# First sweep of a graph layer: two PSUM buffers for the support's product, and the first panel's degrees after fourteen tiles

## The chip, the cores and the metric

The kernel runs on one NeuronCore of a Trainium2 chip. The metric is the device time of one execution in microseconds (us). TensorE is called PE here, VectorE DVE, ScalarE ACT, GpSimd POOL, and SP is the engine whose queue issues nearly all DMAs.

## What is computed

Two graph-and-feed-forward layers on x (3327 rows of 256 fp32 numbers, padded to 26 tiles of 128) with a 3327 by 3327 matrix `adj`. The change lies in the first graph convolution:

```python
def _L0_gnn_ref(x, adj, W):
    A_hat = adj + jnp.eye(adj.shape[0], dtype=adj.dtype)
    d_inv_sqrt = jnp.sum(A_hat, axis=1) ** (-0.5)
    A_norm = d_inv_sqrt[:, None] * A_hat * d_inv_sqrt[None, :]
    support = x @ W.T
    out = A_norm @ support
    return jax.nn.relu(out)
...
x = x + _L0_gnn_ref(_layernorm(x, axis=-1), adj, L0_gnn_W)
```

After it come a routed feed-forward of 8 experts, a second graph convolution, and a feed-forward of 30 steps.

## The kernel before

`first_graph_block` reads the transposed matrix twice. The first sweep, which is where the change is, goes through 9 groups of rows q = 0 to 8 (eight panels of 3 tiles and a last one of 2); each panel has 13 chunks i = 0 to 12 of 384 KB, loaded into a ring `raw` of 11 slots by SP (L381, in `load`). SP issues load n when `free(n - 11)` says that the chunk which last used the slot has been read.

What each engine does in the first sweep, in the order written out in its program:

- DVE adds every chunk of a panel into a PSUM accumulator (`add_chunk`, L583 for a panel's first pair, L586 after that; even panels use `psT[:, 0:2]`, odd ones `acc[1]`). At chunk 4 of panel q it reads the degrees of panel q - 1 (`degrees`, L591 to L594), at chunk 7 it scales three tiles of support (`scale_s`, L600 and L604), and for chunks whose rows have been scaled it makes the low half of a split (`split_low`, L611).
- ACT copies a finished accumulator to `colsum` (`column_sum`, L459), makes the high halves (`split_high`, L473) and keeps a panel's partial product (`keep_part`, L468).
- PE turns the column sums into degrees (`degrees`, L908, and L911 where PE has added some chunks itself, L921), and multiplies split chunks by scaled support (`contract`, L931).
- POOL takes the power -0.5 of the degrees (`invert`, L842).

Beside this, during panels 0 and 1, the support is made, one tile t after another, by ACT and PE in turns. Step t of `support_steps` is: ACT normalises tile t (`normalise_x`, L441), copies the transposed tile t - 1 out of PSUM (`copy_xnT`, L448), and copies the product of tile t - 2 to `s_row` (`copy_support`, L452). PE transposes tile t (`turn_x`, L891), and multiplies tile t - 1 by the weights (`support`, L901). The transposes have two PSUM buffers (`psX`), the product has one (`psS`, in the bank of `psR`):

```python
                if t >= 1:
                    pe.wait_ge(sup_done, t)
                for k in range(KD):
                    last = pe.matmul(psS, xnT[:, t % 2, k, :], w[:, k, :], start=(k == 0), stop=(k == KD - 1))
```

so PE's product of tile t waits until ACT has copied that of tile t - 1. Steps 0 to 17 belong to panel 0, steps 18 to 27 to panel 1's chunks 0 to 9. ACT takes panel 0's `column_sum` at chunk 1 of panel 1 (behind step 18), PE its `degrees` at chunk 2 (behind step 19, which multiplies tile 18). Contraction of panel 1 begins at its chunk 11, on PE behind a wait for all 26 tiles of support, and on ACT (L473) behind the last copy of support.

Of the kernel before, what the change touches and what calls it, by code (L numbers as in the profile page):

```python
# [25 lines left out]
ACT = mybir.ActivationFunctionType  # L26
# [7 lines left out]
D = 256  # L34
KD = D // P
# [8 lines left out]
PT = 3  # L44
# [5 lines left out]
CHUNKS = NT // CT  # L50
# [129 lines left out]
def first_graph_block(nc, g, x_in, w0, adjt, adjl, s_row, route):  # L180


    with ExitStack() as ctx:
# [14 lines left out]
        w = sb("g0_w", [P, KD, D])  # L198
        xn = sb("g0_xn", [P, 2, D])
        xnT = sb("g0_xnT", [P, 2, KD, P])  # L200
# [38 lines left out]
        psT = ps("g0_psT", [P, PT, 512])  # L239
        psR = ps("g0_psR", [P, 512])  # L240
# [1 line left out]
        deg_acc = [psT[:, 0:CT, :], acc[1]]  # L242
        psD = psT[:, PT - 1, 0:NT]
        psX = [acc[0][:, b, 0:D].rearrange("p (k n) -> p k n", k=KD) for b in range(2)]
        psS = psR[:, 0:D]
        psP = psR[:, 0:PANEL]

        filled, placed = sem("filled"), sem("placed")
# [5 lines left out]
        xn_done, xtr_done, xnT_done, xmm_done, sup_done = (sem(n) for n in ("xn", "xtr", "xnT", "xmm", "sup"))  # L254
        dve_added, pe_added = sem("dve_added"), sem("pe_added")
        colsum_done, deg_mm, deg_added, deg_done = sem("colsum"), sem("deg_mm"), sem("deg_added"), sem("deg")
# [12 lines left out]
        def tiles_of(q):  # L269
            return list(range(q * PT, min(q * PT + PT, NT)))  # L270
# [30 lines left out]

        def support_steps(q, i):
            if q == 0:
                return [i] if i < 8 else [2 * i - 8, 2 * i - 7]
            return [18 + i] if q == 1 and i < 10 else []


        def part_of(q):
# [12 lines left out]
        def item(q, i):  # L321
            return q * CHUNKS + i
# [40 lines left out]
        def early_before(q, i):  # L363
            return before1(q) + sum(len(early(q, a)) for a in range(i))
# [71 lines left out]
        def _(act):  # L436
# [12 lines left out]

            def copy_support(t):  # L450
                act.wait_ge(xmm_done, t + 1)
                act.activation(s_row[:, t, :], psS, ACT.Copy).then_inc(sup_done, 1)  # L452

            def column_sum(q):
                v = width(q)
# [51 lines left out]
            for q in range(GROUPS):  # L507
                for i in range(CHUNKS):
                    n = item(q, i)
                    if i == 1 and q >= 1:  # L510
                        column_sum(q - 1)
                    if i == 2 and q >= 2:
                        keep_part(q - 1)
                    if early(q, i):
                        act.wait_ge(loaded[n % RING], n // RING * 16 + 16)
                    for a, j in enumerate(early(q, i)):
                        split_high(early_before(q, i) + a, n, j % CT, width(q))
                    for t in support_steps(q, i):
                        if t < NT:
                            normalise_x(t)  # L520
                        if 1 <= t <= NT:
                            copy_xnT(t - 1)
                        if t >= 2:
                            copy_support(t - 2)
# [360 lines left out]
        def _(pe):  # L885
# [8 lines left out]
            def support(t):  # L894
                if t == 0:
                    pe.wait_ge(w_loaded, 16)
                pe.wait_ge(xnT_done, t + 1)
                if t >= 1:
                    pe.wait_ge(sup_done, t)
                for k in range(KD):  # L900
                    last = pe.matmul(psS, xnT[:, t % 2, k, :], w[:, k, :], start=(k == 0), stop=(k == KD - 1))  # L901
                last.then_inc(xmm_done, 1)

            def degrees(q):
                pe.wait_ge(colsum_done, q + 1)
                for i, t in enumerate(tiles_of(q)):
                    for a in range(CT):
                        last = pe.matmul(psD[:, t:t + 1], colsum[:, a, i * P:(i + 1) * P], g.ones[:, 0:1], start=(a == 0),  # L908
                                         stop=(a == CT - 1 and not PE_SUMS[q]))
                    if PE_SUMS[q]:  # L910
                        last = pe.matmul(psD[:, t:t + 1], rowsum[0:1, i * P:(i + 1) * P], g.ones[0:1, 0:1], start=False,  # L911
                                         stop=True)
                last.then_inc(deg_mm, 1)
# [61 lines left out]

            for q in range(GROUPS):
                for i in range(CHUNKS):
                    if i == 2 and q >= 1:
                        degrees(q - 1)
                    if i in pe_places(q):  # L980
                        add_chunk(q, i)
                    for a, j in enumerate(early(q, i)):
                        if j == 0 and q >= 2:
                            pe.wait_ge(part_done, q - 1)
                        if j == 0 and q == 1:
                            pe.wait_ge(sup_done, NT)
                        if j % PT == 0:
                            pe.wait_ge(sl_done, j // PT + 1)
                        contract(early_before(q, i) + a, acc[0], j, width(q), j == 0, j == q * PT - 1)
                    for t in support_steps(q, i):  # L990
                        if t < NT:
                            turn_x(t)
                        if 1 <= t <= NT:
                            support(t - 1)
            for m in range(END):
                if m == 1:
                    degrees(GROUPS - 1)
                if m < TURNS:
                    k, j = PLACE[m], row_tile(m)
# [1194 lines left out]
```

## Time and profile before

| | us |
|---|---|
| median of 3 runs | 1946.84 (1945.93 to 1947.46) |
| the profiled execution, its own time | 1950.9 |
| its span | 1949.1 |
| busy in the span: PE, DVE, ACT, POOL | 1807.9, 1616.5, 1331.3, 959.1 |
| issued loads of `raw` in panels (384 KB), number and median time to landing | 168, 4.8 |

The profile gives for each engine its busy time, and a trace of every instruction with what ended the idle time before it. The first sweep of the first graph layer fills roughly the first 218 us of the span. A matrix product that the program issues once stands as two matmuls in the trace (fp32), so the two products of one tile are four L901 rows. "Granted clock" is the share of full speed that PE's clock was let run at.

### The profile page before, as it was taken

How to read it: one execution, taken by the hardware profiler on the slowest of the kernel's cores; microseconds unless marked ns; L12 is line 12 of the kernel's file. 1: busy time of each engine (PE TensorE's matmuls, PEld its weight loads, DVE VectorE, ACT ScalarE, POOL GpSimd, SP SyncE). 2: the span in 40 equal slices, each digit the busy share in tenths (PEclk: the TensorE clock that was granted, in tenths of full speed). 3: DMA queues.
4: the chain of work that ended last, by engine and by line, in shares of the span. 5: the costliest groups of instructions: out<-in, count | busy, mean ns of one | idle time of the engine just before them, and what ended most of it. 6: DMA issues, size and time to landing. Idle time of an engine off the chain costs nothing. (4 is left out here: it accounts for less than half of the span.)

```text
span 1949.1 us, 41788 instructions
## 1 busy us (share of the span) xinstructions
PE 1807.9 (93%) x12680; PEld 1702.0 (87%) x12680; DVE 1616.5 (83%) x4226; ACT 1331.3 (68%) x2651; POOL 959.1 (49%) x1703
## 2 busy tenths in 40 slices
PE   6799999829999999858999979999999999999997
PEld 4689999829999999857888869999999999999997
DVE  5689878739999999738656559999999999999996
ACT  4434555416666666543555459999999999999995
POOL 2000134535555555530101027777777777777774
PEclk8889999959999999979999999999999999999999
DMA  8676778237887887543556400000000000000002
GB/s 310 207 250 201 218 200 179 96 136 215 233 234 232 236 237 228 133 170 104 193 173 203 143 17 2 2 2 2 2 1 2 2 2 2 2 2 2 2 2 71
DMA packets 97235, 226.26 MB, mean 116 GB/s; under 512 B 20897, under 2 KB 51363, under 8 KB 88620
## 3 DMA queue, kind: packets, MB, share of 16 engines
q1 hardware_dynamic: 82476, 206.33, 33.8%
q0 software_dynamic: 14592, 17.91, 4.7%
q8 instruction: 80, 1.31, 0.3%
q14 instruction: 87, 0.71, 0.1%
HBM read 204.43 MB, written 19.75 MB: 115 GB/s over the span
## 5 line engine op out<-in xcount | busy, mean ns | idle before, releaser
L2028 PE MATMUL ffn_psH<-ffn_w2h,ffn_vTh 128*128 128x256 f32 x1320 | 393.0, 298 | 1.5 <-DVE ffn_u L2084 1.5
L2028 PE MATMUL ffn_psH<-ffn_w2h,ffn_vTl 128*128 128x256 f32 x1320 | 374.3, 284 | 0.0
L2028 PE MATMUL ffn_psH<-ffn_w2l,ffn_vTh 128*128 128x256 f32 x1320 | 373.9, 283 | 0.0
L2117 POOL TENSOR_SCALAR ffn_vn<-ffn_vn,ffn_rstd,ffn_shift 128x256 f32<-128x256 f32 x540 | 300.0, 560 | 21.1 <-issue 1.2
L2072 DVE BATCH_NORM_STATS2 ffn_stats<-ffn_vn 128x6 f32<-128x256 f32 x780 | 284.5, 406 | 25.0 <-ACT ffn_vn L2054 23.9
L2084 DVE SCALAR_TENSOR_TENSOR ffn_u<-ffn_th,ffn_psH 128x512 f32<-128x512 f32 x390 | 263.5, 676 | 7.4 <-ACT ffn_th L2051 7.4
L2028 PEld LDWEIGHTS ffn_psH<-ffn_w2h,ffn_vTh 128*128 128x128 f32 x1320 | 253.0, 192 | 2.5 <-DVE ffn_u L2084 1.7
L2028 PEld LDWEIGHTS ffn_psH<-ffn_w2l,ffn_vTh 128*128 128x128 f32 x1320 | 253.2, 192 | 0.8
L2028 PEld LDWEIGHTS ffn_psH<-ffn_w2h,ffn_vTl 128*128 128x128 f32 x1320 | 252.5, 191 | 0.0
L2054 ACT ACTIVATE ffn_vn<-ffn_u 128x512 f32<-128x512 f32 x390 | 248.7, 638 | 0.8 <-DVE ffn_u L2084 0.8
L2051 ACT ACTIVATE ffn_th<-ffn_psH 128x512 f32<-128x512 f32 x390 | 232.6, 596 | 1.7 <-PE ffn_psH L1991 1.7
L2077 DVE TENSOR_TENSOR ffn_vTl<-ffn_psT,ffn_vTh 128x512 fp32r<-128x512 f32 x330 | 222.1, 673 | 3.6 <-ACT ffn_vTh L2045 3.6
L2009 PE MATMUL ffn_psT<-ident,ffn_vn 128*128 128x128 f32 x1560 | 214.7, 275 | 10.0 <-POOL ffn_vn L2117 9.8
L2045 ACT ACTIVATE ffn_vTh<-ffn_psT 128x512 fp32r<-128x512 f32 x330 | 195.9, 594 | 27.1 <-PE ffn_psH L2028 17.2
L2009 PEld LDWEIGHTS ffn_psT<-ident,ffn_vn 128*128 128x128 f32 x1560 | 175.0, 141 | 27.4 <-POOL ffn_vn L2117 23.1
L1738 ACT ACTIVATE moe_hr<-moe_psH,moe_b 128x256 f32<-128x256 f32 x264 | 110.8, 471 | 126.0 <-PE moe_psH L1846 117.0
L2123 POOL TENSOR_TENSOR ffn_rstd<-ffn_veps,mhalf 128x4 f32<-128x4 f32 x195 | 196.4, 1007 | 0.1
L931 PE MATMUL g_acc<-g_hi,g_sh 128*128 128x384 f32 (+1 forms) x468 | 162.6, 347 | 12.0 <-DVE g_lo L611 6.8
L473 ACT ACTIVATE g_hi<-g_raw 128x384 fp32r<-128x384 f32 (+1 forms) x234 | 111.6, 508 | 88.7 <-PE g_acc L931 71.5
L1364 DVE TENSOR_TENSOR g_lo<-g_raw,g_hi 128x512 fp32r<-128x512 f32 (+1 forms) x182 | 114.3, 649 | 67.2 <-ACT g_hi L1307 66.8
L1307 ACT ACTIVATE g_hi<-g_raw 128x512 fp32r<-128x512 f32 (+1 forms) x182 | 105.2, 597 | 91.1 <-PE g_acc L1492 90.1
L2060 ACT ACTIVATE ffn_vn<-ffn_vn,ffn_shift,ffn_rstd 128x256 f32<-128x256 f32 x240 | 144.4, 602 | 26.7 <-POOL ffn_shift L2127 24.5
(240 smaller groups left out, 5021.6 us busy)
## 6 DMA issues: line engine op xcount, KB each, us to landing
g_raw<-in_adjt SPq DMA_DIRECT2D x168, 384.0 KB, 4.8
g_raw<-in_wide SPq DMA_DIRECT2D x78, 512.0 KB, 3.7
moe_w1raw<-in_wall SPq DMA_DIRECT2D x33, 1024.0 KB, 5.2
moe_w2raw<-in_wall SPq DMA_DIRECT2D x33, 1024.0 KB, 5.9
moe_b<-in_eb SPq DMA_DIRECT2D x33, 128.0 KB, 4.5
g_raw<-in_adjl SPq DMA_DIRECT2D x14, 256.0 KB, 2.8
g_raw<-in_narrow SPq DMA_DIRECT2D x13, 256.0 KB, 2.6
xn_rows<-rt_hn SPq DMA_DIRECT2D x8, 384.0 KB, 4.2
```

Source lines behind the costliest of these rows:

```text
L931: last = pe.matmul(to[:, d, 0:v], s[:, j, fs], a[:, b, 0:v], start=(first and r == 0), stop=(last_one and r == 2))
L2009: last = pe.transpose(psT[w % R][:, q * KD + k, :], vn[:, gr * Q + q, k * P:(k + 1) * P], g.ident[:])
L2028: last = pe.matmul(psH[w % R][:, q * D:(q + 1) * D], a[:, w % R, q * KD + k, :], b[:, k, :], start=(k == 0 and j == 0), stop=(k == KD - 1 ...
L2045: act.activation(to[:, m % R], psT[m % R][:], ACT.Copy).then_inc(copied, 1)
L2051: act.activation(th[:, a], psH[a][:], ACT.Tanh).then_inc(th_done, 1)
L2054: act.activation(vn[:, tiles(m - SILU)].rearrange("p q d -> p (q d)"), u[:, (m - SILU) % R], ACT.Silu).then_inc(v_done, 1)
L2060: act.activation(vn[:, t, :], vn[:, t, :], ACT.Identity, scale=rstd[:, s:s + 1], bias=shift[:, s:s + 1]).then_inc(vn2_done, 1)
L2072: last = dve.bn_stats(stats[:, t, :], vn[:, t, :])
L2077: dve.tensor_tensor(vTl[:, w % R], psT[w % R][:], vTh[:, w % R].bitcast(F32), ALU.subtract).then_inc(lo_done, 1)
L2084: dve.scalar_tensor_tensor(out=u[:, a], in0=th[:, a], scalar=0.01, in1=psH[a][:], op0=ALU.mult, op1=ALU.add).then_inc(u_done, 1)
L2117: last = pool.tensor_scalar(vn[:, t, :], vn[:, t, :], rstd[:, s:s + 1], shift[:, s:s + 1], ALU.mult, ALU.add)
L2123: pool.tensor_tensor(rstd[:, q], veps[:, q], g.mhalf[:, 0:2 * Q], ALU.pow).then_inc(rstd_done, 1)
```

## The change

The product of the support gets a second PSUM buffer, `psS = (psR[:, 0:D], psT[:, PT - 1, D:2 * D])`; even tiles use the first, odd tiles the second, and PE's product of tile t waits for ACT's copy of tile t - 2 in place of t - 1. The second buffer lies in the bank in which `psD`, the degrees, lies. For that, PE takes the degrees of panel 0 only when 14 tiles (0 to 13) have been copied, and the product of an odd tile from 15 on waits until DVE has read those degrees. Step 13 and 14 now come at chunk 0 of panel 1, two steps a chunk go on to chunk 3, and one a chunk to chunk 10. ACT takes panel 0's `column_sum` at chunk 0 of panel 1, ahead of step 13, and PE takes its degrees at chunk 1, behind step 14. In the new file the lines of the support and of what follows stand 6 to 10 lines further down.

```diff
--- before.py
+++ after.py
@@ -242,7 +242,8 @@
         deg_acc = [psT[:, 0:CT, :], acc[1]]
         psD = psT[:, PT - 1, 0:NT]
         psX = [acc[0][:, b, 0:D].rearrange("p (k n) -> p k n", k=KD) for b in range(2)]
-        psS = psR[:, 0:D]
+
+        psS = (psR[:, 0:D], psT[:, PT - 1, D:2 * D])
         psP = psR[:, 0:PANEL]
 
         filled, placed = sem("filled"), sem("placed")
@@ -301,8 +302,13 @@
 
         def support_steps(q, i):
             if q == 0:
-                return [i] if i < 8 else [2 * i - 8, 2 * i - 7]
-            return [18 + i] if q == 1 and i < 10 else []
+                return [i]
+            if q == 1 and i < 11:
+                return [CHUNKS + 2 * i, CHUNKS + 2 * i + 1] if i < 4 else [CHUNKS + 4 + i]
+            return []
+
+
+        AHEAD_OF_DEGREES = CHUNKS + 1
 
 
         def part_of(q):
@@ -449,7 +455,7 @@
 
             def copy_support(t):
                 act.wait_ge(xmm_done, t + 1)
-                act.activation(s_row[:, t, :], psS, ACT.Copy).then_inc(sup_done, 1)
+                act.activation(s_row[:, t, :], psS[t % 2], ACT.Copy).then_inc(sup_done, 1)
 
             def column_sum(q):
                 v = width(q)
@@ -507,7 +513,7 @@
             for q in range(GROUPS):
                 for i in range(CHUNKS):
                     n = item(q, i)
-                    if i == 1 and q >= 1:
+                    if i == (0 if q == 1 else 1) and q >= 1:
                         column_sum(q - 1)
                     if i == 2 and q >= 2:
                         keep_part(q - 1)
@@ -895,14 +901,18 @@
                 if t == 0:
                     pe.wait_ge(w_loaded, 16)
                 pe.wait_ge(xnT_done, t + 1)
-                if t >= 1:
-                    pe.wait_ge(sup_done, t)
+                if t >= 2:
+                    pe.wait_ge(sup_done, t - 1)
+                if t % 2 and t >= AHEAD_OF_DEGREES:
+                    pe.wait_ge(deg_added, 1)
                 for k in range(KD):
-                    last = pe.matmul(psS, xnT[:, t % 2, k, :], w[:, k, :], start=(k == 0), stop=(k == KD - 1))
+                    last = pe.matmul(psS[t % 2], xnT[:, t % 2, k, :], w[:, k, :], start=(k == 0), stop=(k == KD - 1))
                 last.then_inc(xmm_done, 1)
 
             def degrees(q):
                 pe.wait_ge(colsum_done, q + 1)
+                if q == 0:
+                    pe.wait_ge(sup_done, AHEAD_OF_DEGREES)
                 for i, t in enumerate(tiles_of(q)):
                     for a in range(CT):
                         last = pe.matmul(psD[:, t:t + 1], colsum[:, a, i * P:(i + 1) * P], g.ones[:, 0:1], start=(a == 0),
@@ -975,7 +985,7 @@
 
             for q in range(GROUPS):
                 for i in range(CHUNKS):
-                    if i == 2 and q >= 1:
+                    if i == (1 if q == 1 else 2) and q >= 1:
                         degrees(q - 1)
                     if i in pe_places(q):
                         add_chunk(q, i)
```

PE's order before, around the degrees of panel 0 (L891 the transposes, L901 the product, L908 the degrees; each row with "x5" or without is so many instructions, and `g_psR` is the PSUM tile of the product):

```order
L901 MATMUL g_psR<-g_w,g_xnT 128x256 [waits g0_sup,g0_xnT]
L901 MATMUL g_psR<-g_w,g_xnT 128x256
L908 MATMUL g_psT<-ones,g_colsum 128x1 [waits g0_colsum]
L908 MATMUL g_psT<-ones,g_colsum 128x1 x5
L891 MATMUL g_acc<-ident,g_xn 128x128 [waits g0_xnT,g0_xn]
L891 MATMUL g_acc<-ident,g_xn 128x128
L901 MATMUL g_psR<-g_w,g_xnT 128x256 [waits g0_sup,g0_xnT]
L901 MATMUL g_psR<-g_w,g_xnT 128x256
```

The same place in the changed kernel (L897 the transposes, L909 the product, L918 the degrees):

```order
L909 MATMUL g_psT<-g_w,g_xnT 128x256 [waits g0_sup,g0_xnT]
L909 MATMUL g_psT<-g_w,g_xnT 128x256
L918 MATMUL g_psT<-ones,g_colsum 128x1 [waits g0_sup,g0_colsum]
L918 MATMUL g_psT<-ones,g_colsum 128x1 x5
L897 MATMUL g_acc<-ident,g_xn 128x128 [waits g0_xnT,g0_xn]
L897 MATMUL g_acc<-ident,g_xn 128x128
L909 MATMUL g_psR<-g_w,g_xnT 128x256 [waits g0_sup,g0_xnT]
L909 MATMUL g_psR<-g_w,g_xnT 128x256
L897 MATMUL g_acc<-ident,g_xn 128x128 [waits g0_xnT,g0_xn]
L897 MATMUL g_acc<-ident,g_xn 128x128
L909 MATMUL g_psT<-g_w,g_xnT 128x256 [waits g0_deg_added,g0_sup,g0_xnT]
L909 MATMUL g_psT<-g_w,g_xnT 128x256
```

The degrees stood behind the products of 19 tiles and now stand behind those of 14, with a wait for their copies; the products alternate between two tiles of PSUM, and that of tile 15 has a further wait for DVE's reading of the degrees.

ACT's order in the changed kernel, at the boundary from panel 0 to panel 1 (L447 normalises, L454 copies the transposes, L458 the product, L465 the column sums):

```order
L447 ACTIVATE g_xn<-x,g_negshift,g_rstd 128x256 [waits g0_xtr,g0_norm0]
L454 ACTIVATE g_xnT<-g_acc 128x256 [waits g0_xmm,g0_xtr]
L458 ACTIVATE l_s<-g_psR 128x256 [waits g0_xmm]
L465 ACTIVATE g_colsum<-g_psT 128x768 [waits g0_dve_added]
L447 ACTIVATE g_xn<-x,g_negshift,g_rstd 128x256 [waits g0_xtr,g0_norm0]
L454 ACTIVATE g_xnT<-g_acc 128x256 [waits g0_xmm,g0_xtr]
L458 ACTIVATE l_s<-g_psT 128x256 [waits g0_xmm]
```

Before, the copy of the column sums stood behind 19 normalised tiles (0 to 18); now it stands behind 13 (0 to 12), and still waits for DVE's last addition of panel 0. The orders of DVE, POOL and SP are the same in both kernels.

## Rows read from the trace of the kernel before

**Rows 1.** Windows: length, busy PE, PEld, DVE, ACT, POOL; granted clock, DMA share, GB/s

```profile
19.80:29.80 10.00, 9.08 (x23) 6.06 (x24) 7.62 (x31) 5.19 (x14) 0.85 (x1) 0.50 1.03 406
29.80:49.00 19.20, 15.37 (x71) 11.07 (x69) 10.54 (x11) 12.78 (x34) 4.18 (x11) 1.00 0.80 278
49.00:66.00 17.00, 12.71 (x62) 9.31 (x62) 9.63 (x18) 10.97 (x29) 0.85 (x1) 1.00 0.45 139
74.50:77.60 3.10, 3.10 (x11) 3.10 (x10) 3.06 (x8) 0.56 (x2) 0.00 (x0) 0.50 0.49 138
88.00:101.50 13.50, 12.49 (x39) 11.18 (x40) 9.14 (x19) 4.27 (x9) 0.85 (x1) 0.50 0.88 309
```

**Rows 2.** Waits from 28 to 66: us in total, times, longest

```profile
PE g_psR L901 <- ACT l_s L452: 6.6, 19, 0.6
```

**Rows 3.** Timeline of DVE: start, us, work, count, [idle before and its releaser]

```profile
28.77 8.46 DVE L586 TENSOR_TENSOR g_psT<-g_psT,g_raw 128x768 f32<-128x768 f32 x8
...
53.43 0.16 DVE L591 TENSOR_SCALAR g_deg<-g_psT 128x3 f32<-128x3 f32 x1 [12.12 <-PE g_psT L908]
...
58.88 4.17 DVE L586 TENSOR_TENSOR g_acc<-g_acc,g_raw 128x768 f32<-128x768 f32 x4
65.40 1.03 DVE L611 TENSOR_TENSOR g_lo<-g_raw,g_hi 128x384 fp32r<-128x384 f32 x2 [2.35 <-ACT g_hi L473]
...
90.05 0.97 DVE L583 TENSOR_TENSOR g_acc<-g_raw 128x768 f32<-128x768 f32 x1 [7.07 <-issue]
```

**Rows 4.** Timeline of ACT

```profile
30.46 0.38 ACT L452 ACTIVATE l_s<-g_psR 128x256 f32<-128x256 f32 x1 [1.08 <-PE g_psR L901]
30.74 0.59 ACT L441 ACTIVATE g_xn<-x,g_negshift,g_rstd 128x256 f32<-128x256 f32 x1
31.24 0.37 ACT L448 ACTIVATE g_xnT<-g_acc 128x256 f32<-128x256 f32 x1
...
49.08 0.81 ACT L459 ACTIVATE g_colsum<-g_psT 128x768 f32<-128x768 f32 x1
49.77 0.60 ACT L441 ACTIVATE g_xn<-x,g_negshift,g_rstd 128x256 f32<-128x256 f32 x1
...
64.57 0.38 ACT L452 ACTIVATE l_s<-g_psR 128x256 f32<-128x256 f32 x1 [1.28 <-PE g_psR L901]
64.85 1.34 ACT L473 ACTIVATE g_hi<-g_raw 128x384 fp32r<-128x384 f32 x3
```

**Rows 5.** Timeline of PE

```profile
20.31 0.69 PE L891 MATMUL g_acc<-ident,g_xn 128*128 128x128 f32 x2 [3.94 <-ACT g_xn L441]
...
23.55 2.04 PE L901 MATMUL g_psR<-g_w,g_xnT 128*128 128x256 f32 x4
25.39 0.63 PE L891 MATMUL g_acc<-ident,g_xn 128*128 128x128 f32 x2
...
30.99 1.10 PE L901 MATMUL g_psR<-g_w,g_xnT 128*128 128x256 f32 x4 [0.35 <-ACT l_s L452]
31.93 0.38 PE L891 MATMUL g_acc<-ident,g_xn 128*128 128x128 f32 x2
...
52.00 1.40 PE L908 MATMUL g_psT<-ones,g_colsum 128*128 128x1 f32 x12
53.25 0.42 PE L891 MATMUL g_acc<-ident,g_xn 128*128 128x128 f32 x2
53.50 1.03 PE L901 MATMUL g_psR<-g_w,g_xnT 128*128 128x256 f32 x4
54.37 0.38 PE L891 MATMUL g_acc<-ident,g_xn 128*128 128x128 f32 x2
...
63.43 1.10 PE L901 MATMUL g_psR<-g_w,g_xnT 128*128 128x256 f32 x4 [0.56 <-ACT l_s L452]
...
73.95 0.41 PE L931 MATMUL g_acc<-g_hi,g_sh 128*128 128x384 f32 x1 [1.94 <-DVE g_lo L611]
```

**Rows 6.** Loads of L381 that were issued from 0 to 90

```profile
DMA to landing us min/median/max: 3.1/8.1/13.9
```

## The prediction

> **What bounds the kernel now.** I read the timelines of DVE, ACT and PE over the first 90 us first, since the change touches only panels 0 and 1 of the first sweep, then the windows for the clock and the transfers, and last the loads. The question is which chain ends last before the first contraction on PE, because from there on all engines wait for one another.
>
> It is the chain of the support. DVE is through with panel 0 at 28.77 + 8.46 = 37.23, adds four more times, and then stands idle for 12.12 us, until 53.43, for the degrees, which PE makes behind the products of 19 tiles [rows 3, 5]. It is still not the one that is late: from 53.43 it has 9.6 us of work (to 58.88 + 4.17 = 63.05), and then waits another 2.35 us for ACT's high halves [rows 3], which ACT begins behind its last copy of support, at 64.57 [rows 4]. So the two waits are 14.5 us of idle DVE, but the chain of the support decides the moment 65.40 at which the work of panel 1 goes on.
>
> That chain runs in turns. PE waits 19 times, 6.6 us in all, for ACT's copy of the product [rows 2]. One turn: the copy starts at 30.46 and takes 0.38, the product starts 0.15 later at 30.99 and takes 1.10 [rows 4, 5], and the next copy starts 0.04 after it (63.43 + 1.10 = 64.53, copy at 64.57). Sum 0.38 + 0.15 + 1.10 + 0.04 = 1.67 us a tile. The transfers do not bind here: the queues fall from 278 to 139 GB/s in the second half of this stretch, as DVE frees no slot while it waits [rows 1].
>
> **The change, part by part.**
>
> *Two buffers.* The product of a tile no longer waits for the copy just before. Three bounds are left. PE alone: transposes at 53.25, product at 53.50, next transposes at 54.37, 1.12 us a tile [rows 5] (the other product rows give 31.93 - 30.99 = 0.94 in place of 0.87, so up to 1.19). ACT alone: 0.28 from copy to normalising, 0.50 from there to the copy of the transposes [rows 4], and some 0.28 for that one, 1.06. The loop through both over two tiles: 0.28 + 0.50 + 0.37 + 0.15 + 1.10 + 0.04 = 2.44, that is 1.22 us a tile. It is the longest of the three, so I take 1.22; 1.12 stays as the lower end, 1.67 (nothing gained) as the upper. At the low clock, where a product with its gap takes 25.39 - 23.55 = 1.84 and the transposes some 0.5 (twice 0.25), a tile takes 2.34.
>
> *Before the hand-over this is worth nothing on the path.* ACT now copies the column sums ahead of step 13, and that copy waits for DVE, whose end at 37.23 nothing moves. With 1.22 us a tile, ACT and PE have done steps 0 to 12 by about 37.2 (PE's transposes of tile 7 about 29.6, five more steps bring 35.9, the product behind them ends about 37.3); so the support arrives there as DVE ends. ACT waits some 1 us and PE some 1.3 us for it. This is a new wait, and behind it on ACT stand step 13 and all later ones: it is what the 5 tiles gained so far are spent on.
>
> *From the hand-over on.* Column sums 37.25, normalising 0.69 later at 37.94 (49.77 - 49.08 [rows 4]), copy of tile 12's transposes at 38.44, end 38.81, product of tile 12 at 38.96; product of tile 13 after 0.94 and 0.25 at 40.15, end 41.25, its copy 41.29 to 41.67; degrees on PE at 41.82. They hold PE for 53.25 - 52.00 = 1.25 us, and DVE reads them 1.43 us after their start (53.43 - 52.00), so at 43.25, **10.2 us earlier** than before. DVE is ready then (it has waited since 41.3), so the new wait of tile 15's product on DVE's reading, done at 43.4, is over before PE is there (tile 14's product starts at 43.32 and takes longer). I cost it at nothing; the cover is tile 14's product, and if it were gone the price would be some 0.2 us, once.
>
> *The rest of the support.* Product of tile 14 at 43.32, eleven more at 1.22 put that of tile 25 at 56.7, end 57.8, its copy 57.9 to 58.2, where it was 64.57 to 64.95. **The chain ends 6.7 us earlier.** With 1.12 a tile it would be 7.8, with 1.35 5.3.
>
> *DVE.* Degrees at 43.25 plus 9.6 us gives 52.9; it then waits about 5.9 us for ACT's high halves in place of 2.35. So 10.2 us come on DVE, 3.5 of them are given back in this wait, and 6.7 stay. Its additions need chunks that landed before 46, and slots freed earlier let SP issue its next loads 10 us earlier, in a stretch where the queues have room [rows 1]; the next slot that SP needs is then one that only the contraction frees. SP and POOL have the same order as before; POOL's powers have tens of us of slack.
>
> *After that* every engine stands where it stood at 65.40, 6.7 us earlier, with the same loads in the ring; what follows is the same sequence. Sum: -6.7 us. The profiled execution took 1950.9 us (span 1949.1), which would make 1944.2; it lay 4.1 us above the median of the runs, so against the median of 1946.84 the forecast is **1940.1 us**. A measurement of this kernel can tell about 0.2% from no change, 3.9 us.
>
> **A rule that speaks against it.** The rows say that PE waits for the copies, 0.35 us a tile [rows 5], at full clock. The Trainium skill (TensorE: Matmul & The Clock Gate, section HAM oscillation — how this bites in real kernels) reports of a matmul kernel, once its loop order was mended, that double-buffering PSUM gave no further gain. By that the sum would be 0 and the time 1946.8; this trace, with 6.6 us of such waits, disagrees, and the case that no gain comes is rival E.
>
> **The rivals.**
>
> *A. The clock halves at the new hand-over.* After 3.94 us of idle PE ran at 0.50 (its level of 1.2 GHz) for 10 us, after 1.94 us for 3.1 us, and once for 13.5 us [rows 1, 5]. The new gaps are 1.3 us and 0.6 us: against. Price: in a low stretch a tile takes 2.34 in place of 1.22, so 48% of it is lost: 1.5 us for 3.1, 4.8 for 10, 6.5 for 13.5. Time 1941.6 to 1946.6, at its middle 1945.
>
> *B. It ends slower.* The mechanism is the same, but kept up: PE's short gaps between products keep its clock at 1.2 GHz to the end of the support. From tile 12's product at 38.96, thirteen more tiles at 2.34 (30.4), 2.5 for the degrees, about 0.5 for their wait and 2.5 from the last product's start to its copy's end bring 74.9, 9.9 us later than 64.95: 1957. It decides from a low stretch of 6.7 / 0.48 = 14 us on. Against: from 29.8 to 66 the clock was 1.00 with larger gaps than the change leaves [rows 1]. The Trainium skill (TensorE: Matmul & The Clock Gate, section A second HAM failure mode: psum-queue depth-cycling) tells of a kernel whose cycling through PSUM banks made the clock swing between its levels in just this way; no row here shows it.
>
> *C. The transfers take it back.* At 83 to 90 DVE waits 7.07 us [rows 3] for chunks that took up to 13.9 us to land [rows 6]. If they came at the same moment as before, all 6.7 us would go into a longer wait: 1946.8. Against: SP issues them as slots come free, and that moves too.
>
> *D. More than the sum.* The low stretch from 88 to 101.5, in which PE is busy for 12.49 of 13.50 us [rows 1], falls otherwise or is shorter; at full clock up to half of that busy time goes, of which DVE would see perhaps 4 us: 1936.
>
> *E. It doesn't do what it says:* another wait keeps a tile at 1.67; only the degrees move, DVE waits for ACT instead, 1946.8.
>
> **How the numbers follow.** Forecast 0.65 (its own range 1938.5 to 1942, from 1.12 and 1.35 us a tile and the scatter of the runs), A 0.12, B 0.04, C 0.07, D 0.08, E 0.04. Faster by over 0.2% (below 1942.9): forecast, D and a quarter of A, 0.76. Same: most of A, C and E, 0.20. Slower: B, 0.04. The range leaves out B, most of C and E, and the ends of A and D: 1936 to 1945.
>
> **What would show it.** In the changed profile: products of the support 1.2 us apart with no wait for the copy two before; DVE's degrees at about 43; the last copy of support at about 58; DVE's first low half near 58.8 after a wait of about 6 us; and PE's clock at 1.00 from 30 to 59. Every later landmark, the wait for chunks at 83 to 90 first, should stand 6 to 7 us earlier. The forecast is wrong if tiles stay above 1.4 us apart, if the clock falls at 38 to 45, or if the wait for chunks grows by what was gained.

## The result, and the profile after

| | before | changed |
|---|---|---|
| median, us (lowest to highest) | 1947.03 (1943.36 to 1949.59, 20 runs) | 1942.66 (1939.01 to 1948.35, 20 runs) |
| ratio | | 0.9981, 95% interval 0.9974 to 0.9989 |
| profiled execution, its span, us | 1950.9, 1949.1 | 1943.88, 1942.1 |

The change gains 4.4 us by the medians (2.1 to 5.1 by the interval). It is faster beyond doubt, but at 0.19% it sits right at the bound of what one measurement tells. The forecast was a gain of 6.7 us and 1940.1 us. One thing is odd at once: the changed kernel scatters over 9.3 us, and the kernel before over 6.2.

Lines of the changed kernel stand 6 to 10 further down than in the rows of before: product L909, PE's transposes L897, degrees L918, ACT's copy of the support L458, high halves L479, DVE's low halves L617. The timeline of PE (start, us, work, [idle before and its releaser]), from the first tiles to the end of the support, answers to [rows 5]:

```profile
20.47 0.69 PE L897 MATMUL g_acc<-ident,g_xn 128*128 128x128 f32 x2 [4.70 <-ACT g_xn L447]
...
33.60 0.38 PE L897 MATMUL g_acc<-ident,g_xn 128*128 128x128 f32 x2
33.81 1.03 PE L909 MATMUL g_psT<-g_w,g_xnT 128*128 128x256 f32 x4
38.78 0.44 PE L897 MATMUL g_acc<-ident,g_xn 128*128 128x128 f32 x2 [3.93 <-ACT g_xn L447]
39.05 1.46 PE L909 MATMUL g_psR<-g_w,g_xnT 128*128 128x256 f32 x4
40.30 0.64 PE L897 MATMUL g_acc<-ident,g_xn 128*128 128x128 f32 x2
40.73 1.91 PE L909 MATMUL g_psT<-g_w,g_xnT 128*128 128x256 f32 x4
43.21 1.47 PE L918 MATMUL g_psT<-ones,g_colsum 128*128 128x1 f32 x12 [0.56 <-ACT l_s L458]
...
45.88 1.03 PE L909 MATMUL g_psT<-g_w,g_xnT 128*128 128x256 f32 x4
46.78 0.44 PE L897 MATMUL g_acc<-ident,g_xn 128*128 128x128 f32 x2
47.06 1.13 PE L909 MATMUL g_psR<-g_w,g_xnT 128*128 128x256 f32 x4
48.02 0.38 PE L897 MATMUL g_acc<-ident,g_xn 128*128 128x128 f32 x2
48.24 1.03 PE L909 MATMUL g_psT<-g_w,g_xnT 128*128 128x256 f32 x4
...
57.48 1.03 PE L909 MATMUL g_psT<-g_w,g_xnT 128*128 128x256 f32 x4
```

Two tiles take 48.24 - 45.88 = 2.36 us, 1.18 each, and no product waits for a copy any more. But at the hand-over PE stands idle for 3.93 us, and the two products behind that take 1.46 and 1.91 us and not 1.03 to 1.13. From 44.50 to 57.50 PE is busy for all of the 13.00 us: now PE itself sets the 1.18 us a tile. In the first stretch tile 7 is turned at 27.62, 2.0 us earlier than I forecast. The windows (busy PE, PEld, DVE, ACT, POOL; then granted clock, DMA share, GB/s) show why:

```profile
34.00:39.30 5.30, 1.37 (x7) 0.84 (x7) 4.88 (x6) 2.05 (x6) 0.31 (x1) 1.00 0.97 319
39.30:42.60 3.30, 3.30 (x10) 2.11 (x9) 1.96 (x3) 1.87 (x5) 0.00 (x0) 0.56 0.96 352
44.50:57.50 13.00, 13.00 (x69) 10.12 (x69) 9.04 (x16) 11.07 (x30) 0.85 (x1) 1.00 0.72 238
88.00:101.50 13.50, 13.50 (x56) 12.42 (x56) 12.18 (x24) 4.35 (x9) 0.85 (x1) 0.77 0.71 242
```

Behind the idle time the clock is granted at 0.56, which is nearly all at the lower level of 1.2 GHz, and then it is back. ACT's timeline has the other side of the same wait, for DVE's sums of panel 0, and the end of the support, [rows 4]:

```profile
33.80 0.38 ACT L458 ACTIVATE l_s<-g_psR 128x256 f32<-128x256 f32 x1
37.43 0.81 ACT L465 ACTIVATE g_colsum<-g_psT 128x768 f32<-128x768 f32 x1 [3.25 <-DVE g_psT L592]
...
58.54 0.38 ACT L458 ACTIVATE l_s<-g_psT 128x256 f32<-128x256 f32 x1 [0.48 <-PE g_psT L909]
58.82 1.34 ACT L479 ACTIVATE g_hi<-g_raw 128x384 fp32r<-128x384 f32 x3
```

And DVE's timeline, [rows 3]:

```profile
28.93 8.46 DVE L592 TENSOR_TENSOR g_psT<-g_psT,g_raw 128x768 f32<-128x768 f32 x8
...
44.71 0.16 DVE L597 TENSOR_SCALAR g_deg<-g_psT 128x3 f32<-128x3 f32 x1 [3.25 <-PE g_psT L918]
...
50.17 4.17 DVE L592 TENSOR_TENSOR g_acc<-g_acc,g_raw 128x768 f32<-128x768 f32 x4
59.37 1.03 DVE L617 TENSOR_TENSOR g_lo<-g_raw,g_hi 128x384 fp32r<-128x384 f32 x2 [5.03 <-ACT g_hi L479]
...
83.80 0.97 DVE L589 TENSOR_TENSOR g_acc<-g_raw 128x768 f32<-128x768 f32 x1 [6.87 <-issue]
```

The degrees come 8.7 us earlier than in [rows 3], the first low half 6.0 (65.40 to 59.37), and the wait for chunks in panel 3 has moved along by 6.2 and is as long as it was.

### The profile page after: what moved, and what is told of

Its sections match the earlier page's. It is cut to its first block and busy times, and to the rows that moved or that the text cites. A ratio compares the mean times of both kernels' runs of the same rounds, so it can differ in the third digit from the quotient of the medians.

```text
span 1942.1 us, 41788 instructions
## 1 busy us (share of the span) xinstructions
PE 1801.2 (93%) x12680; PEld 1698.4 (87%) x12680; DVE 1616.5 (83%) x4226; ACT 1330.7 (69%) x2651; POOL 961.5 (50%) x1703
## 5 line engine op out<-in xcount | busy, mean ns | idle before, releaser
L479 ACT ACTIVATE g_hi<-g_raw 128x384 fp32r<-128x384 f32 (+1 forms) x234 | 111.6, 508 | 88.1 <-PE g_acc L941 70.8
```

## The experiments

Three questions: which half of the change (two buffers, or the earlier hand-over, where ACT takes panel 0's column sums and PE its degrees) brings the gain; whether the idle time at the hand-over costs, by the clock or by the wait itself; and why the gain is smaller than the 6.0 us by which the landmark (DVE's first low half) moved. Each edit is shown against the changed kernel, with what it leaves alone marked by `...`.

**The order alone** (one buffer, the early hand-over):

```
-        psS = (psR[:, 0:D], psT[:, PT - 1, D:2 * D])
+        psS = (psR[:, 0:D], psR[:, 0:D])
...
-                if t >= 2:
-                    pe.wait_ge(sup_done, t - 1)
-                if t % 2 and t >= AHEAD_OF_DEGREES:
-                    pe.wait_ge(deg_added, 1)
+                if t >= 1:
+                    pe.wait_ge(sup_done, t)
...
-                if q == 0:
-                    pe.wait_ge(sup_done, AHEAD_OF_DEGREES)
```

> The change with one PSUM buffer for the product: column sums ahead of step 13 on ACT, degrees behind 14 tiles, but PE waits for the copy just before, 1.67 us a tile. Theory (the two buffers bring the whole gain, the order none): degrees read by DVE near 45.5, but last copy of support at 64.9 and first low half at 65.4 as before, and a median within 1.5 us of the kernel before. Rival (the order brings part of the gain, as DVE's additions and SP's loads come 8 us sooner): median 2 us or more below before.

Measured: 1945.78 us against 1945.38 before, ratio 1.0003 (0.9994 to 1.0011): no gain. DVE has its degrees at 42.78, 2.7 us earlier than expected, and hands all of it back in the wait for ACT. (Its first low half is at 63.08 and not at the expected 65.4; that is a matter of where this execution began the support, see the table below.)

```profile
42.78 0.16 DVE L597 TENSOR_SCALAR g_deg<-g_psT 128x3 f32<-128x3 f32 x1 [2.93 <-PE g_psT L914]
...
63.08 1.03 DVE L617 TENSOR_TENSOR g_lo<-g_raw,g_hi 128x384 fp32r<-128x384 f32 x2 [10.68 <-ACT g_hi L479]
```

**The buffers alone** (the old steps, column sums and degrees at their old places), twice:

```
-                return [i]
-            if q == 1 and i < 11:
-                return [CHUNKS + 2 * i, CHUNKS + 2 * i + 1] if i < 4 else [CHUNKS + 4 + i]
-            return []
+                return [i] if i < 8 else [2 * i - 8, 2 * i - 7]
+            return [18 + i] if q == 1 and i < 10 else []
-        AHEAD_OF_DEGREES = CHUNKS + 1
+        AHEAD_OF_DEGREES = 19
...
-                    if i == (0 if q == 1 else 1) and q >= 1:
+                    if i == 1 and q >= 1:
...
-                    if i == (1 if q == 1 else 2) and q >= 1:
+                    if i == 2 and q >= 1:
```

> Two buffers, hand-over where it stood before (column sums behind step 18 on ACT, degrees behind step 19 on PE). Theory (the support now reaches the new hand-over 3.3 us before DVE, so ACT and PE stand idle there, 3.25 and 3.93 us, and the clock falls after it): with no such idle time the tiles run through at 1.17 us, degrees read by DVE near 46, last copy of support near 55, first low half near 55.6 (59.4 in the changed kernel), no low clock between 30 and 55, and a median near 1938, 4 us below the changed kernel. Rival (the early hand-over is what brings the gain, as in the prediction): DVE gets its degrees later than 50, and the median is 1943 or more.

Measured: 1937.56 us, ratio 0.996 (0.9947 to 0.9974), that is 8.5 us below before and more than the whole change brings. PE has no idle time of 3 to 4 us: the largest in this stretch are 0.38 before tile 19's turn and 0.57 before the degrees, and the first low half starts at 55.97. One thing expected did not hold: the clock fell all the same, at 45.5, for 3.4 us.

```profile
42.04 0.44 PE L895 MATMUL g_acc<-ident,g_xn 128*128 128x128 f32 x2 [0.38 <-ACT g_xn L445]
```

```profile
45.52 0.16 DVE L595 TENSOR_SCALAR g_deg<-g_psT 128x3 f32<-128x3 f32 x1 [3.94 <-PE g_psT L916]
...
55.97 1.03 DVE L615 TENSOR_TENSOR g_lo<-g_raw,g_hi 128x384 fp32r<-128x384 f32 x2 [0.83 <-ACT g_hi L477]
```

So the two buffers carry the gain, and the earlier hand-over costs a part of it.

**The hand-over three steps later** (behind step 15 rather than step 12; the rest as changed):

```
-                return [i]
+                return [i] if i < 10 else [2 * i - 10, 2 * i - 9]
             if q == 1 and i < 11:
-                return [CHUNKS + 2 * i, CHUNKS + 2 * i + 1] if i < 4 else [CHUNKS + 4 + i]
+                return [16, 17] if i == 0 else [17 + i]
...
-        AHEAD_OF_DEGREES = CHUNKS + 1
+        AHEAD_OF_DEGREES = 17
```

> Hand-over three tiles later than in the change (column sums ahead of step 16 on ACT, degrees behind 17 tiles and step 17). Theory: ACT and PE wait less than 0.7 us at the hand-over, degrees read by DVE near 43.6, last copy of support near 55, first low half near 55.5, median near 1938, equal to the kernel with buffers alone. Rival (the place of the hand-over is indifferent): as the changed kernel, 1942 to 1943.

Measured: 1938.3 us, ratio 0.9959 (0.9945 to 0.9973). The idle time of 3.93 us has become 0.39, the first low half is at 55.14, and the clock stays at 1.00:

```profile
39.26 0.44 PE L897 MATMUL g_acc<-ident,g_xn 128*128 128x128 f32 x2 [0.39 <-ACT g_xn L447]
```

```profile
38.00:43.00 5.00, 4.05 (x23) 2.94 (x22) 3.46 (x4) 4.47 (x12) 0.00 (x0) 1.00 0.94 349
43.00:57.00 14.00, 12.36 (x67) 9.78 (x67) 10.88 (x20) 9.73 (x26) 0.85 (x1) 1.00 0.78 266
```

**The idle time filled** (the changed order; PE repeats its two transposes of tile 12 fourteen times in place of standing idle, so the wait for DVE is still there, but PE is busy in it; the helper `transposes` takes the tile, the number of times and whether to signal, and its definition is left out here):

```
+                        if t == CHUNKS - 1:
+                            transposes(t, 14, True)
```

> The changed kernel with 13 more transposes of tile 12 on PE, in the time in which PE waits for the hand-over (about 3.1 us of work in 3.9 us of idle time), the same values written again. Theory (the clock falls after the idle time and this costs about 1.5 us in the profiled run, more in the third of the executions that lie near 1947): clock 1.00 from 38 to 43, first low half near 58 in place of 59.4, median near 1939.5, and the executions near 1947 become rare. Rival (the slow third comes from elsewhere): the median falls by 1.5 us or less and the spread stays at 9 us.

Measured: 1939.1 us, ratio 0.9965 (0.9952 to 0.9979). PE is busy for 3.22 us of the wait, 0.64 remains, and the clock does not fall:

```profile
34.68 3.22 PE L900 MATMUL g_acc<-ident,g_xn 128*128 128x128 f32 x28
38.54 0.44 PE L900 MATMUL g_acc<-ident,g_xn 128*128 128x128 f32 x2 [0.64 <-ACT g_xn L447]
38.82 1.13 PE L913 MATMUL g_psR<-g_w,g_xnT 128*128 128x256 f32 x4
```

```profile
38.00:58.00 20.00, 17.79 (x94) 13.80 (x94) 12.19 (x21) 16.29 (x45) 0.86 (x1) 1.00 0.74 269
```

**The changed kernel and the one before, again.** One profile each is not enough in a stretch where the clock swings, so both were profiled again.

> The changed kernel once more, for its spread and a second profile. Theory: two groups of executions, near 1940 and near 1947; if this profile lies in the upper one, the low clock behind the hand-over or later in the first sweep lasts longer than the 3.3 us of the first profile. Rival: one group around 1942.7, the two groups were chance.

Measured: 1942.99 us, ratio 0.9989 (0.9978 to 0.9999). Four of 11 executions lie from 1945.33 up; the profiled one, 1942.99, shows a fall of 3.4 us behind 4.29 us of idle time.

> The kernel before once more, for a second profile of it. Theory (the execution profiled first lay high by chance, and part of its excess over the median lies in the stretch to 237 us, in the clock behind the wait for chunks): first low half again at 65.4, PE's first transposes of the result (g_out_t) at 233 to 235 in place of 237.0, time within 1 us of the median of the other runs. Rival: 237 again, the difference between the gain of the profiles (7.0) and of the medians (4.4) comes from behind the first graph layer.

Measured: 1946.6 us, ratio 1.0003 (0.9994 to 1.0012), as it must be. Its profile took 1944.75 us, 6.1 less than the one on which the prediction was built, and the difference lies in the stage that the change touches:

```profile
49.62 0.16 DVE L591 TENSOR_SCALAR g_deg<-g_psT 128x3 f32<-128x3 f32 x1 [10.08 <-PE g_psT L908]
61.60 1.03 DVE L611 TENSOR_TENSOR g_lo<-g_raw,g_hi 128x384 fp32r<-128x384 f32 x2 [2.35 <-ACT g_hi L473]
```

```profile
19.00:23.00 4.00, 3.68 (x10) 2.67 (x11) 2.71 (x7) 1.94 (x6) 0.00 (x0) 0.57 1.04 417
23.00:61.00 38.00, 30.38 (x144) 21.96 (x142) 24.46 (x52) 24.87 (x65) 5.88 (x12) 1.00 0.75 268
```

The first low half is at 61.60, not at 65.40. PE began tile 3 at 18.54 in place of 20.31, and the clock was low for 3.4 us in place of 10 [rows 1]. My expectation of 65.4 for it was wrong.

> The changed kernel a third time, beside the kernel before and the order alone on the same chip. Theory (scatter of the clock behind the hand-over and in the first sweep): first low half between 59.3 and 59.8 whenever the low stretch there is 3.3 us, later by 0.5 us for each us that it is longer; median 3 to 5 us below before. Rival: first low half the same to 0.2 us in all profiles, so that the scatter of 9 us comes wholly from later stages.

Measured: 1940.65 us, ratio 0.9975 (0.9963 to 0.9987). Its profiled execution took 1946.08 us and shows what the others don't: the clock stays low for 13.5 us behind the idle time, to the middle of the second panel's support.

```profile
37.09 0.69 PE L897 MATMUL g_acc<-ident,g_xn 128*128 128x128 f32 x2 [4.39 <-ACT g_xn L447]
37.57 1.91 PE L909 MATMUL g_psR<-g_w,g_xnT 128*128 128x256 f32 x4
...
39.70 1.91 PE L909 MATMUL g_psT<-g_w,g_xnT 128*128 128x256 f32 x4
42.18 2.69 PE L918 MATMUL g_psT<-ones,g_colsum 128*128 128x1 f32 x12 [0.56 <-ACT l_s L458]
```

```profile
36.00:49.50 13.50, 11.85 (x39) 9.58 (x40) 7.78 (x14) 6.11 (x16) 0.86 (x1) 0.51 0.75 271
```

```profile
61.96 1.03 DVE L617 TENSOR_TENSOR g_lo<-g_raw,g_hi 128x384 fp32r<-128x384 f32 x2 [7.43 <-ACT g_hi L479]
```

By now 43 executions of the changed kernel lay in two bands, up to about 1942 and from 1943 on, with five of them close about that bound (1942.76 to 1943.10). The last measurement put it beside its two counterparts on one chip.

> The changed kernel once more, beside the two that follow on the same chip. Its 43 executions so far lie in two bands, about 1937 to 1942 and 1943 to 1948. My theory: the upper band is executions whose clock stays at its lower level for long after the new idle time at the hand-over (36 to 50 us in the one profile that took 1946.1), so both bands should show again, with a median of 1940 to 1943. A rival: the bands are the scatter that every kernel has; then the next two kernels should scatter as widely, over 8 us or more.

Measured: 1941.19 us, ratio 0.998 (0.9968 to 0.9992). Nine of 12 lie between 1938.13 and 1942.88, three between 1947.58 and 1948.48.

> Two buffers with the old order of the hand-over, once more. My theory: it has no idle time of 3 to 4 us on PE at 37, so no execution lies in the upper band: median 1937 to 1939, all below 1942. If the early hand-over costs nothing and the difference seen before was chance, its median stands within 2 us of the changed kernel's.

Measured: 1939.65 us (1937.32 to 1941.67), ratio 0.9963 (0.995 to 0.9976). None in the upper band; the median is 0.7 above what I expected, and in this measurement only 1.5 below the changed kernel's, which by my own bound of 2 us would leave the rival standing. In the first pair of measurements the distance was 5.4 us, and over all executions (below) it is 3.0.

> The changed order with PE's idle time at the hand-over filled by repeated transposes of tile 12 (the same values, written again). My theory, the clock: no upper band, median 1938 to 1940.5, granted clock 1.00 from 30 to 58. The rival, that the wait itself costs (ACT and PE stand for DVE) and not the clock: it should look as the changed kernel does, upper band included, since the wait for DVE is still there.

Measured: 1941.36 us (1937.89 to 1943.12, 8 runs), ratio 0.9968 (0.9958 to 0.9979): the median is 0.9 above the expected span, and no lower than that of the changed kernel in the same measurement, 1941.19. The earlier pair had 1939.1 against 1942.99. So the medians leave the price of the fall at anything from nothing to 3.9 us. The granted clock reads 1.00 throughout this stretch, as expected, and even in the one before it:

```profile
19.00:36.00 17.00, 15.32 (x78) 12.28 (x79) 13.77 (x38) 11.25 (x30) 5.54 (x14) 1.00 0.98 363
36.00:58.00 22.00, 19.12 (x107) 14.91 (x105) 14.10 (x23) 16.95 (x45) 0.85 (x1) 1.00 0.79 273
```

For the earlier stretch the instructions contradict that column. Two products there take as long as they do at the lower level in the other profiles:

```profile
20.84 1.91 PE L913 MATMUL g_psR<-g_w,g_xnT 128*128 128x256 f32 x4
...
22.97 1.41 PE L913 MATMUL g_psT<-g_w,g_xnT 128*128 128x256 f32 x4
```

From 24.43 on every product takes 1.03 to 1.13, so behind the hand-over the clock was up by both signs.

All executions together, from every measurement:

| | executions | median, us | above 1943 | from 1945 up |
|---|---|---|---|---|
| before | 95 | 1946.3 | 89 | 68 |
| order alone | 11 | 1945.8 | 11 | 6 |
| changed | 55 | 1941.9 | 22 | 17 |
| idle time filled | 13 | 1940.1 | 1 (1943.12) | 0 |
| two buffers alone | 10 | 1938.9 | 0 | 0 |
| hand-over behind step 15 | 5 | 1938.3 | 0 | 0 |

The gap in the changed kernel's executions lies between 1943.88 and 1945.33, and the first profiled execution, 1943.88, shows the short fall, so the last column is the better count: 38 executions below it with a median of 1940.7, 17 above with 1947.55. Were the bands the same for all, none of these 17 would fall among the 28 of the last three kernels about three times in 10,000. Within the two measurements that had both, the counts are 4 of 11 against 0 of 15 and 3 of 12 against 0 of 13, which chance alone would bring about twice in 1,000 (all worked out from the counts). So the upper band belongs to the idle time at the hand-over.

The granted clock of whole executions points the same way: it is 0.962 to 0.965 in the 17 (mean 0.9631) and 0.965 to 0.971 in the 38 (mean 0.9667). By an estimate, a difference of 0.0036 over 1945 us is some 14 us more at half the clock. It doesn't say where in the execution they lie, and a mean of 0.964 alone does not put an execution into the upper band: one of each of the other three kernels has it, at 1941.57 to 1942.95.

Where each profiled execution stood, in us (the turn of g_out_t is PE's first transposes of the layer's result; DVE's idle time before the landmark in brackets; the last column is the span less the column before it):

| | execution | PE's turn of tile 3 | degrees read | first low half | first turn of g_out_t | rest |
|---|---|---|---|---|---|---|
| before | 1950.9 | 20.31 | 53.43 [12.12] | 65.40 [2.35] | 237.0 | 1712.1 |
| before again | 1944.75 | 18.54 | 49.62 [10.08] | 61.60 [2.35] | 232.2 | 1710.8 |
| order alone | 1946.05 | 18.83 | 42.78 [2.93] | 63.08 [10.68] | 233.2 | 1711.1 |
| changed | 1943.88 | 20.47 | 44.71 [3.25] | 59.37 [5.03] | 229.8 | 1712.3 |
| again | 1942.99 | 20.59 | 45.05 [3.49] | 59.71 [5.04] | 229.9 | 1711.3 |
| third | 1946.08 | 18.79 | 44.91 [5.13] | 61.96 [7.43] | 233.3 | 1711.0 |
| fourth | 1941.95 | 20.10 | 44.47 [3.39] | 59.13 [5.03] | 228.6 | 1711.6 |
| filled | 1940.07 | 20.24 | 43.10 [1.87] | 57.76 [5.04] | 226.6 | 1711.7 |
| filled again | 1943.12 | 20.36 | 43.24 [1.87] | 57.90 [5.03] | 228.1 | 1713.3 |
| buffers alone | 1937.21 | 20.58 | 45.52 [3.94] | 55.97 [0.83] | 225.4 | 1710.1 |
| and again | 1941.67 | 20.12 | 45.28 [4.18] | 56.82 [1.92] | 227.9 | 1712.0 |
| hand-over 16 | 1941.57 | 20.78 | 43.82 [2.05] | 55.14 [1.71] | 226.8 | 1713.0 |

From the first low half to the turn of g_out_t it is 168.8 to 171.7 us everywhere, and the rest is 1710.1 to 1713.3: what the change gains or loses is settled by the first low half, and some 3 us of scatter in either stretch come on top, whatever the kernel. (So the hand-over behind step 15 has the earliest landmark, 55.14, and an execution of 1941.57.)

The column of tile 3's turn matters too. Three of these executions began it at 18.5 to 18.8, the others at 20.1 to 20.8, and DVE's sums of panel 0 moved with it (they end at 35.5 and 35.7 in the second profile of before and the third of the changed kernel, at 37.2 and 37.4 in the first ones). So landmarks are compared from tile 3's turn. From there the first low half comes 45.1 and 43.1 us later in the kernel before, 44.3 in the order alone, 38.9 to 39.1 in the changed kernel's three short cases, 43.2 in its long one, 37.5 with the idle time filled, 35.4 and 36.7 with the buffers alone, and 34.4 with the hand-over behind step 15.

**The constants.** In every kernel above DVE stands idle for some 7 us in panel 3. Behind it are four small transfers (zeros, the slot table, two router tensors) that SP issues between the loads of panels 2 and 3. One edit, on top of the two buffers alone, moves them a panel ahead, between the loads of panels 1 and 2:

```
-                if q == 2:
+                if q == 1:
                     constants()
```

> Two buffers with the hand-over where it stood before (as the kernel e1), and SP issues the four small transfers of constants behind panel 1's loads in place of panel 2's, near 39 to 43 us, where DVE waits for its degrees. Theory (DVE's wait of 7 us for chunks in panel 3 comes from these transfers, which stand ahead of panel 3's first loads): the wait of 6.99 us at 80.5 falls under 2 us, and the median lies 4 to 6 us below e1, near 1933. Rival (the wait comes from the ring, whose slots come free late in panel 2): it stays at 5 us or more and the median within 1.5 us of e1.

Measured: 1929.9 us, ratio 0.9918 (0.9905 to 0.9931), 7.7 below the same kernel without the edit (6.9, when each is taken against the kernel before of its own measurement), and 3 us lower than I expected. The wait of 7 us is gone; one of 1.77 us at 57.85 is new. DVE's timeline, first of the kernel with the buffers alone, then of this one:

```profile
80.54 0.97 DVE L587 TENSOR_TENSOR g_acc<-g_raw 128x768 f32<-128x768 f32 x1 [6.99 <-issue]
```

```profile
57.85 0.97 DVE L587 TENSOR_TENSOR g_psT<-g_raw 128x768 f32<-128x768 f32 x1 [1.77 <-issue]
...
72.02 0.96 DVE L587 TENSOR_TENSOR g_acc<-g_raw 128x768 f32<-128x768 f32 x1
```

Of the 8.5 us between the two starts 2.1 are the earlier turn of tile 3 in this execution (18.45 for 20.58), so the edit is worth some 6.4 there. The two summaries of the transfers from 60 to 80 us, the same two kernels in the same order, say what filled the time:

```profile
DMA packets 2260, 4.69 MB, mean 235 GB/s; under 512 B 594, under 2 KB 850, under 8 KB 2259
```

```profile
DMA packets 2304, 6.32 MB, mean 316 GB/s; under 512 B 252, under 2 KB 252, under 8 KB 2303
```

As many packets, but a third more bytes: with the constants in this stretch many of the packets are small. Which of the four transfers it is, and whether their packets or their issue on SP (3.4 us from 61.76 to 65.18) cost more, I did not try apart.

**The best of both** (hand-over behind step 15, constants early):

> The hand-over behind step 15 (e3_handover_16) and the four small transfers of constants a panel earlier (e8_constants_early). If the two gains stand beside each other: 1938.3 less the 7.7 us between e8 and e1, about 1930.6, no wait of 7 us at 80. If the constants only helped with the old order of the hand-over: about 1938.

Measured: 1931.01 us, ratio 0.9917 (0.9904 to 0.993), 7.3 below the hand-over behind step 15 without the edit (8.2, each against its own before), as expected, and the wait of 7 us is gone here too. It does no better than the buffers alone with constants early: that one is 15.5 us and this one 16.0 us below the kernel before the change, each in its own measurement.

## Why the prediction was right, and where it was off

**Two buffers make a tile take 1.22 us and not 1.67: right.** Measured 1.18. But the bound was misnamed: PE is busy for 13.00 of 13.00 us there, so it is PE alone (1.12 to 1.19 in my own working) and not the loop through ACT (1.22). What the Trainium skill reports of its kernel (TensorE: Matmul & The Clock Gate, section HAM oscillation — how this bites in real kernels), that double-buffering PSUM gave no further gain, does not carry over to this one: alone it brings 0.996 and 0.9963, the largest effect of the change. Rival E is out.

**The support's chain decides, not the degrees: right, and shown.** With the order alone the degrees come 6.8 us earlier than in the profile of before that began tile 3 at nearly the same time (42.78 for 49.62), and nothing is gained.

**"Before the hand-over this is worth nothing on the path": right, with a price that I missed.** The step that failed is the one behind it: the support "arrives there as DVE ends", so that ACT waits some 1 us and PE 1.3. It arrived 3.3 us early. I had taken over the low clock up to 29.8 from the one profile; in the changed kernel the clock was up at 26, which brought tile 7's turn 2.0 us forward, and 1.18 us a tile did the rest. ACT waited 3.25 to 3.95 us, and PE 3.93, 4.29, 4.39 and 4.30 in the four profiles. This opened rival A, which I had priced well (a gain cut to 1941.6 to 1946.6) and given only 0.12 on the ground of gaps that were three times too small. The clock fell in all four profiles: for 3.4 us in three, for some 13.5 in the third.

**What the fall costs.** From tile 3's turn to the first low half, the short case takes 38.9 to 39.1 us and the filled kernel 37.5: 1.4 to 1.6 us. The long case takes 43.2, which is 5.6 more than the filled kernel. Rival A had 1.5 for 3.1 us of low clock and 6.5 for 13.5, so its prices were near. The long case stands 4.1 to 4.3 us behind the short one; the bands are 6.8 apart. That the upper band of executions is this long case rests on one profile of it, on this size, which covers the greater part of the distance, and on the granted clocks above; the rest of the distance has no source on record. That the band is absent without the idle time rests on 28 executions. The filled kernel still waits for DVE's sums, and its first low half comes 0.9 to 2.8 us behind those of the kernels that hand over later: the wait itself costs too, and no less than a short fall.

**The sum of 6.7 us: mis-sized by where it was measured from.** The landmark came out near what I had (58.8 forecast; 59.1 to 59.7 in three profiles), and the profiled execution of the changed kernel took 1943.88 us where the sum made 1944.2. But I carried the sum over to the medians as if the 4.1 us by which that profile of before lay above its median would be in the changed kernel too. Part of them lay inside this very stage: 10 us of low clock against 3.4 in the second profile, and a tile 3 that began 1.8 us later. The two are not alike. The later start is one that either kernel feels, since DVE's sums move with it. The longer low clock, some 2.0 us of the landmark (45.1 less 43.1), is one that the changed kernel does not feel: it lies ahead of the hand-over, where ACT and PE have 3 to 4 us to spare. So, from tile 3's turn, the change gains 6.0 to 6.2 us in the short case against the profile on which the prediction was built, 3.9 to 4.2 against the second one, and against that one nothing in the long case (43.2 for 43.1). The gain of the medians, 4.4, is a mixture of these. That the landmark came out so near its 58.8 is in part luck: without the fall it stands at 57.8 and 57.9 (filled kernel), 0.9 to 1.0 earlier than I had, and the fall that I had not counted put it back by some 1.5.

**DVE's new wait of 5.9 us for the high halves:** 5.03, and 7.43 in the long case. **The degrees at 43.25:** 44.5 to 45.1, late by the low clock; 43.10 and 43.24 in the filled kernel, where it stayed up, so the turn-by-turn sum was right.

**Rival C** (the loads take it back) is out: the wait of 7.07 us became 6.87 and stands 6.2 us earlier. **Rival D:** the stretch from 88 to 101.5 had a clock of 0.77 for 0.50 [rows 1], but between panel 3 and the first turn of g_out_t the profiles show no more than 1 us from it (83.80 to 229.8 is 146.0; 90.05 to 237.0 was 147.0). **Rival B** needed a low clock for 14 us and more without a return; the longest was some 13.5, after which it rose in the middle of the support. It was nearer than its chance of 0.04 said.

## What to carry to other kernels

A wait that a faster chain runs into is new idle time, and its length has to be worked out with the clock at both levels: here some 4 us of it on TensorE, with the fall of the clock behind it, gave back about 3 of the 7 us that the second buffer had earned, and with a hand-over three steps later that loss is gone. Try the part that removes the wait alone before the part that re-times what follows. Where the changed stage has stretches of low clock, take two or more profiles of before, line them up at one early event (here tile 3's turn), and ask of every us that one lies above the median whether the changed kernel would feel it at all.

## What was not expected of the hardware

- Behind 3.93 to 4.39 us of idle TensorE the granted clock was about 0.5 in all four profiles. In the first the turn at 38.78 still took 0.44 us and only the products behind it slowed; in the third and fourth the turn itself took 0.69. The same kernel then ran low for 3.4 us or for 13.5. What decides between them no run here shows.
- Idle time of 0.39 to 1.34 us at the same place left the clock at 1.00 in the filled kernel and in that with the hand-over behind step 15; with the buffers alone it fell at 44 to 45 all the same, behind no more than 0.57 us of idle time and the twelve narrow products of the degrees, for 3.4 and for 6.8 us, and with the constants early at 43, for 3.4. The hand-over behind step 15 has the same twelve products behind 0.56 us and stayed at 1.00. So idle time is not all that brings it down, and what does there stays open.
- The granted clock of a profile can miss a low stretch: in the second profile of the filled kernel it reads 1.00 from 19 to 36, while the products at 20.84 and 22.97 took 1.91 and 1.41 us and those from 24.43 on 1.03 to 1.13. The durations have to be read beside it.
- Moving four small transfers a panel ahead took 7 to 8 us off the kernel's time, more than the change that was studied.
